# Parts of queries and keys stored once in memory, and picked for the stacks by the loads

## The reference

```python
q, k, v = (heads(w, b) for w, b in ((wq, bq), (wk, bk), (wv, bv)))   # 16 heads of D = 16
q, k = _apply_rope(q, cos, sin), _apply_rope(k, cos, sin)            # turns the two halves of D
att = softmax(causal(einsum('bhtd,bhsd->bhts', q, k) / sqrt(D)))
y = einsum('bhts,bhsd->bhtd', att, v)
x = layernorm(x + y @ wp.T + bp)
x = layernorm(x + experts(x))      # 32 experts, 8 of them per token, weighted
```

## Time and profile before

| | |
|---|---|
| median of 3 runs | 2250.6 us (2250.48 to 2256.99) |
| the profiled execution | span 2243.6 us; no other time of it is given |
| TensorE matmuls busy | 1846.1 us (82%) |
| VectorE busy | 1604.2 us (71%) |
| ScalarE busy | 1324.9 us (59%) |
| GpSimd busy | 1247.5 us (56%) |
| DMA, all queues | 520.20 MB in 290572 packets, mean 232 GB/s |
| granted TensorE clock, mean | 0.918 |

### The profile page before, as it was taken

The page is one execution under the profiler, slowest core; times in us unless marked ns, Lnnn a source line. Parts: engine busy times, 40 slices in busy tenths (PEclk is TensorE's granted clock), DMA queues, the critical chain, the costliest instruction groups (busy, mean ns, idle before and its releaser), DMA issues.

```text
span 2243.6 us, 54153 instructions
## 1 busy us (share of the span) xinstructions
PE 1846.1 (82%) x17104; PEld 1323.3 (59%) x17104; DVE 1604.2 (71%) x3572; ACT 1324.9 (59%) x2865; POOL 1247.5 (56%) x1206
## 2 busy tenths in 40 slices
PE   4898888998889888988878989899878889887740
PEld 2555554555545454555446878787767777776630
DVE  4888877887788777877854545575467778776688
ACT  1566565655554554655446767777766667775630
POOL 1004446444644465444644777777777777775660
PEclk7999999999999999999989999999989999998865
DMA  5466577667766876556676766656789988887887
GB/s 164 149 181 222 191 232 248 222 192 227 256 217 200 264 246 226 190 189 222 216 237 219 229 178 214 209 187 199 213 299 307 302 289 299 262 289 266 283 283 256
DMA packets 290572, 520.20 MB, mean 232 GB/s; under 512 B 46329, under 2 KB 192192, under 8 KB 280529
## 3 DMA queue, kind: packets, MB, share of 16 engines
q1 hardware_dynamic: 206400, 324.46, 47.5%
q0 software_dynamic: 58368, 163.70, 19.7%
q10 hardware_dynamic: 25536, 28.58, 3.8%
HBM read 284.54 MB, written 259.20 MB: 242 GB/s over the span
## 4 chain that ended last, share of the span: by engine, by line
PE 39%; DVE 20%; DMA 20%; issue 9%; ACT 5%; SPq 4%; POOL 2%; ACTq 1%; DVEq 1%; POOLq 0%
DMA xTden<-reciprocals 7%; DVE mn L1649 5%; PE ps L1016 4%; PE ps L1094 4%; PE ps L1041 3%; PE ps L1135 3%; PE ps L1067 3%; PE ps L1154 3%; PE ps L1081 3%; PE ps L1137 3%; PE ps L1136 3%; PE ps L1200 2%; PE ps L965 2%; DMA out<-x1T 1%; POOL y_tokens L898 1%
## 5 line engine op out<-in xcount | busy, mean ns | idle before, releaser
L1292 ACT ACTIVATE pT<-ps 128x512 f32<-128x512 f32 (+2 forms) x1008 | 679.5, 703 | 438.3 <-PE ps L1069 315.9
L880 POOL DMA_INDIRECT x_sorted<-xhl,idx x512 | 529.6, 1034 | 508.4 <-DVE xhl L1724 229.3
L1649 DVE TENSOR_REDUCE mn<-ps 128x1 f32<-128x512 f32 (+3 forms) x704 | 412.5, 631 | 55.5 <-PE ps L1043 53.0
L1135 PE MATMUL ps<-pT,gu_hi 128*128 128x256 f16 (+1 forms) x1600 | 383.1, 255 | 23.7 <-ACT pT L1292 12.3
L1136 PE MATMUL ps<-pT,gu_hi 128*128 128x256 f16 (+1 forms) x1600 | 381.9, 254 | 0.0
L1137 PE MATMUL ps<-pT,gu_lo 128*128 128x256 f16 (+1 forms) x1600 | 381.8, 254 | 0.0
L898 POOL DMA_INDIRECT y_tokens<-work,yidx x264 | 283.3, 1073 | 94.8 <-issue 59.1
L1041 PE MATMUL ps<-stacks 96*128 96x512 bf16 (+3 forms) x1024 | 275.4, 312 | 46.6 <-DVE mn L1649 25.4
L1067 PE MATMUL ps<-stacks 99*128 99x512 bf16 (+3 forms) x1024 | 286.5, 311 | 15.1 <-ACT pT L1292 10.1
L1069 PE MATMUL ps<-maskk,identb 128*128 128x128 bf16 x1024 | 223.0, 224 | 0.0
L1200 PE MATMUL ps<-dn,vx 128*128 x608 | 172.0, 283 | 53.0 <-DVE cosT L1857 13.4
(11 more groups left out here) (299 smaller groups left out, 3780.9 us busy)
## 6 DMA issues: line engine op xcount, KB each, us to landing
stacks<-y_tokens SPq DMA_DIRECT2D x64, 1024.0 KB
stacks<-qk_parts SPq DMA_DIRECT2D x128, 384.0 KB
qk_parts<-pbuf SPq DMA_DIRECT2D x62, 384.0 KB
attention<-yev ACTq DMA_DIRECT2D x64, 256.0 KB
qk_parts<-pbuf SPq DMA_DIRECT2D x62, 256.0 KB
stacks<-x_sorted SPq DMA_DIRECT2D x52, 304.0 KB, 4.0
x_sorted<-pads_h SPq DMA_DIRECT2D x99, 152.0 KB
pbuf<-x_sorted SPq DMA_DIRECT2D x40, 304.0 KB
```

The costliest lines, as they stand in the source:

```text
L880: pool.indirect_dma_start(xsort[g][:, :], bass.IndirectOffsetOnAxis(ap=at, axis=0), xhl_rows[:, t, :], None).then_inc(s_scat, 16)
L1135: mmul(o, w_hi[k], x_hi[k], start=k == 0, stop=False)
L1292: return nc.scalar.activation(o, i, f, **k)
L1649: V.tensor_reduce(mn[:, tt, h0:h0 + nh], ps[:, odd_bank("max", at, m), 0:nh * n].rearrange("p (a n) -> p a n", a=nh), axis=AX.X, op=ALU.ma ...
```

## The change

The memory tensor holds the three parts of D = 16 dimensions once, as rows ordered by part, half and j, and in each row the 16 heads side by side. A partition of the tiles is now (j, head) instead of (head, j): weights, biases and the tables of cosines and sines are loaded or built in that order. The parts tile has the part outside and the halves inside; keys have their parts in the reverse order (part_column). One DMA writes the parts of a batch's queries or keys. The stack is loaded by three DMAs of three, two and one part (48, 32 and 16 partitions); for queries they begin at part 0, for keys they end at the last column. A partition's four heads of 512 tokens lie together in memory and in the tile. Counts of s_qkw and s_stk follow.

```diff
-    parts_dram = nc.dram_tensor("qk_parts", [B, 2, H * KS, T], BF16, kind="Internal").ap()
+    parts_dram = nc.dram_tensor("qk_parts", [B, 2, 3 * D, H, T], BF16, kind="Internal").ap()
...
-        pbuf = sb("pbuf", [P, 2, 3, T], BF16)
+        pbuf = sb("pbuf", [P, 3, 2, T], BF16)
...
+        def part_column(n, part):
+
+            return (part, 2 - part)[n]
...
-                        sp.dma_start(dst[:, r:r + 1], src.rearrange("(h r j o) -> r h j o", h=H, r=2, o=1)[r]).then_inc(s_cst, 16)
+                        sp.dma_start(dst[:, r:r + 1], src.rearrange("(h r j o) -> r j h o", h=H, r=2, o=1)[r],
+                                     allow_slow_non_contiguous=True).then_inc(s_cst, 16)
...
-                                 src.rearrange("(h r j) c -> r h j c", h=H, r=2)[r]).then_inc(s_wnat, 16)
+                                 src.rearrange("(h r j) c -> r j h c", h=H, r=2)[r]).then_inc(s_wnat, 16)
...
                 if g == 0:
-                    wait(sp, s_qkw, 192 * (b + 1))
+                    wait(sp, s_qkw, 32 * (b + 1))
                 wait(sp, s_st, NU * (m - 2))
                 for n, dst in enumerate((qs, ks)):
-                    sp.dma_start(dst[0:KS, r, :, :],
-                                 parts_dram[b, n, 4 * KS * g:4 * KS * (g + 1), :].rearrange("(h k) t -> k h t", h=4)).then_inc(s_stk[r], 16)
+                    at = 0
+                    for count in (3, 2, 1):
+                        first = (0, 3 - count)[n]
+                        sp.dma_start(dst[at * D:(at + count) * D, r, :, :],
+                                     parts_dram[b, n, first * D:(first + count) * D, 4 * g:4 * g + 4, :]).then_inc(s_stk[r], 16)
+                        at += count
...
-                runs = (((0, 3, 0), (3, 2, 0), (5, 1, 0)), ((0, 3, 0), (3, 2, 1), (5, 1, 2)))[n]
                 wait(sp, s_pp, 2 * b + n + 1)
-                dst = parts_dram[b, n].rearrange("(p r a) t -> r p a t", r=2, a=6)
-                for half in range(2):
-                    for at, count, part in runs:
-                        src = parts(b, n)[:, half, part:part + count, :] if n == 0 else \
-                            parts(b, n)[:, half, part:part + 1, :].to_broadcast([P, count, T])
-                        sp.dma_start(dst[half][:, at:at + count, :], src).then_inc(s_qkw, 16)
+                sp.dma_start(parts_dram[b, n].rearrange("(q j) h t -> (j h) q t", q=6),
+                             parts(b, n).rearrange("p a r t -> p (a r) t")).then_inc(s_qkw, 16)
...
-                actv(parts(b, n)[:, :, part, :], rotated(b, n)[:, :, :], ACT.Copy).then_inc(s_part, 1)
+                actv(parts(b, n)[:, part_column(n, part), :, :], rotated(b, n)[:, :, :], ACT.Copy).then_inc(s_part, 1)
...
-    rows = np.tile(ang.T, (H, 1))
+    rows = np.repeat(ang.T, H, axis=0)
```

More of the change, by code:

```diff
@@ L452, in build @@
         rcp = prep[:, 3 * C + 3 * E + 4:3 * C + 3 * E + 8].rearrange("p (r m) -> p r m", r=2)
-        first_parts = pT[1][:, :, :].rearrange("p h t -> p (h t)").bitcast(BF16).rearrange("p (r a t) -> p r a t", r=2, a=3)
+        first_parts = pT[1][:, :, :].rearrange("p h t -> p (h t)").bitcast(BF16).rearrange("p (a r t) -> p a r t", r=2, a=3)
         wv_nat, wp_nat = (pT[0][:, k, :].rearrange("p (m c) -> p m c", m=2) for k in range(2))
@@ L461, in build @@
         row_homes = [(qs.rearrange("p r h t -> p (r h t)"), 5), (ks.rearrange("p r h t -> p (r h t)"), 5),
-                     (flat(pT[1][:, :, :]), 2), (pbuf[:, :, :, :].rearrange("p r a t -> p (r a t)"), 2),
+                     (flat(pT[1][:, :, :]), 2), (pbuf[:, :, :, :].rearrange("p a r t -> p (a r t)"), 2),
                      (flat(xTden[:, :, :]), 1), (flat(ynum[:, :, :]), 1), (flat(qf[:, :, :]), 1), (flat(x1[:, :, :]), 1),
@@ L1036, in max_unit @@
                 if m == 0:
-                    wait(pe, s_stk[r], 32 * (at // 3 + 1))
+                    wait(pe, s_stk[r], 96 * (at // 3 + 1))
                 k = odd.take(s_red, NM * at + m + 1, "max", at, m)
@@ L1362, in part_copy @@
                     if b > 0:
-                        wait(act, s_qkw, 96 * at)
+                        wait(act, s_qkw, 16 * at)
                 else:
                     wait(act, s_rest, at + 1)
-                actv(parts(b, n)[:, :, part, :], rotated(b, n)[:, :, :], ACT.Copy).then_inc(s_part, 1)
+                actv(parts(b, n)[:, part_column(n, part), :, :], rotated(b, n)[:, :, :], ACT.Copy).then_inc(s_part, 1)
             def values(b, v):
@@ L1634, in rest @@
                 q = rotated(b, n)[:, :, :]
-                V.tensor_tensor(q, q, parts(b, n)[:, :, 0, :], ALU.subtract).then_inc(s_rest, 1)
+                V.tensor_tensor(q, q, parts(b, n)[:, part_column(n, 0), :, :], ALU.subtract).then_inc(s_rest, 1)
             def last_part(b, n):
@@ L1641, in last_part @@
                 wait(dve, s_part, part_count(b, n, 1))
-                V.tensor_tensor(parts(b, n)[:, :, 2, :], rotated(b, n)[:, :, :], parts(b, n)[:, :, 1, :],
+                V.tensor_tensor(parts(b, n)[:, part_column(n, 2), :, :], rotated(b, n)[:, :, :], parts(b, n)[:, part_column(n, 1), :, :],
                                 ALU.subtract).then_inc(s_pp, 1)
```

## The result

The changed kernel takes 2230.1 us (median of 6 runs) against 2250.7 for the one before (6 runs): ratio 0.9919, 95% interval 0.9894 to 0.9945. In a second comparison, with 10 and 13 runs, it was 2236.2 against 2245.3: 0.9952, interval 0.9921 to 0.9982. Both say faster, by 0.8 and 0.5%; the forecast was 2228 and 2206 to 2247. The forecast gain was 22.7 us. The first comparison shows 20.6 and the second 9.1, less than half of it; over all runs on record, 32 of the kernel before and 16 of the changed one, the means differ by 14 us, give or take 4.

The account below looks back on a forecast made before the run. No engine fills the kernel; late reciprocals, the chain's largest item, hold VectorE's division. Gains of 17.9 + 3.8 - 1 + 2 = 22.7 us off 2250.6 give 2228 us, range 2206 to 2247.

Parts of the forecast that it names:

- Backlog ahead of the numerators: Attention batches: queued writes and loads delay the numerators by 2.2 us; clearing them gives 1.9 a batch, 17.9 us in all.
- the keys' side: Next batch's stack loads go out about 3 us sooner after the keys' halved write; 2 us gained.
- 0.85 and 0.6: Batch time saved per us of less waiting at VectorE's division: 0.85 in the first nine batches, 0.6 in five later.
- rival C: TensorE's clock: moved idle stretches bring slow ones, 2268 us; against it, fewer or shorter slow stretches, 2218; chance 0.07.
- The start: Before the first stack matmul: halved writes land 3.8 us sooner, weights loaded in the new order cost 1 us.
- the weights' order: Queries' and keys' weights read with j ahead of h at the start: 0 to 1.7 us slower, 1 taken.
- The loads: Stack loads by pieces ahead of the numerators: 3.3 us a pair, as before; bounds 2.0 and 6.6 us.
- A: Loads by pieces take 6 us or more a pair and eat the gain, 2249 us; A or nothing: 0.13.
- B: Scatters and weights fill the DMA engines instead; a third of the 17.9 us remains, 2240 us; chance 0.17.
- D: The transfer of 10 us shrinks too and the 14 waits at the division vanish whole, 2210 us; chance 0.08.
- the signs I named: New profile: 241 thousand packets, 495 MB, seven issues before rotation's end, division waits about 30 us, first stacks' wait about 14.
- one sign of being wrong: At the numerators' issue in each batch: the forecast is wrong if 4 KB packets still run then.

Follow-up runs that it names:

- swap2: Changed kernel with the reciprocals' loads issued ahead of the numerators': 2206.3 us, attention phase 1104.1 us.
- rows_1k: Changed kernel with 128 bytes of padding behind each head's row, so loads have 1 KB packets again while writes stay halved: attention phase 1133.6 us.

## Why the prediction was right

The mechanism, a backlog ahead of the numerators, was right and is shown. That the sum came so near is in part luck: sizes inside it were off in opposite directions, and the second comparison gives only 9.1 us. The profiles, from their start to the first expert load, give 20.2 us (1201.2 against 1181.0, means of two).

*Backlog ahead of the numerators, 17.9 us.* The place and the mechanism held. The attention phase is 1154.8 before and 1136.4 after (means of two), 18.4 us less, this term and the keys' side together, of which I had forecast 19.9. But two sizes inside were off, in opposite directions. I took 0.7 us as the shortest time from issue to first packet, from the empty window behind a write's issue (that write's first packet came at 0.87); for these loads it is 1.4, in both kernels' first batch and in twelve of the next thirteen of the changed one. So the shift was not 1.9 us a batch but 1.3, the mean over the 13 batches behind the first (2.75 to 1.45 us), and the waits fell by 13.2 us (means of two), where I had 24 before the factors. Against that, I multiplied by 0.85 and 0.6, each read from one pair of batches, and the phase fell by more than the waits, not less. What the waits don't explain is of the size of a fall in TensorE's busy time. The attention phase in one window, before and after (us, busy and count of PE, PEld, DVE, ACT, POOL, then granted clock, DMA share, GB/s):

```profile
44.50:1200.00 1155.50, 1001.15 (x7935) 591.84 (x7935) 905.75 (x2192) 641.31 (x1248) 509.03 (x507) 0.94 0.66 213
```
```profile
42.90:1178.70 1135.80, 995.36 (x7935) 587.84 (x7935) 905.68 (x2192) 640.76 (x1249) 511.11 (x507) 0.95 0.61 196
```

The same 7,935 matmuls are busy 5.8 us less, at a mean granted clock of 0.95 for 0.94. In swap2 they take 976.4 us at 0.96. The traces' records of the granted clock show as many stretches at 1.2 GHz in the phase as before, 27 and 26 for 26 and 26, but shorter ones: 125 and 117 us in all, for 150 and 141 (swap2: 17 stretches, 81 us). It went the way I had named as the case against rival C, with about half the size. That the clock is the cause of the whole remainder is argued from these rows, not tested by itself.

*The start, 3.8 - 1.* Queries' parts were ready 1.5 us later (issue at 30.92 for 29.39); most of it is the price of the weights' order, for which I had 1 and the wait shows 1.7 in this pair. The two writes landed 5.6 us behind it instead of 9.4: 3.8 us, as forecast. The loads then took 6.4 us to the first stack matmul instead of 5.7, where I had put no change. The sum is 1.6 us sooner in the first pair of profiles, 2.1 in the second, for 2.8. By itself that would prove little, since the same kernel's first stack matmul moves by 3.4 to 3.9 us from one profile to the other; but the 5.6 and 9.4 us repeat in both pairs.

*The loads, 3.3 us a pair.* At 219 GB/s it is 3.6. The Trainium skill's rule of ports (SBUF — State Buffer, Door 1: The DMA port swizzle) would have made it 4.8, an estimate, with the pieces one after another. The rows agree with it in that 96 partitions are filled well below the writes' 384 GB/s, whatever the packet (though these are also loads against writes), and not with most of the further loss: the three pieces seem to overlap for the greater part. Which ports were used isn't shown.

*The keys' side, 2.* The waits for stacks behind the first are 2.2 us for 3.3, so 1.1, and 1.4 for 2.6 in the second pair, 1.2.

*The rivals.* A is out by the issue times and rows_1k. B, that other queues would fill the engines, doesn't show: the first packet comes 1.4 us behind the issue, as into the queue of the first batch, and the transfers did not get longer. They did not get shorter either (9.3 us from the first to the last packet before, 9.5 after, means over 13 batches), so D didn't come. C is out for this change. Of the signs I named, traffic, issues and TensorE's first wait came out. The waits at the division are 42 us where I had said about 30, and the numerators' packets start 1.4 us behind their issue, not 0.7. And one sign of being wrong is there: 4 KB packets still run when the numerators are issued, 34 of them in the batch above and 4 to 97 in each of the first 15. It was too strict a sign. Where fewer than 35 of them are left, the first packet comes at 1.42 to 1.46 us all the same; with 56 and 97 left it comes at 1.52 and 2.66.

## What to carry to other kernels

Find the transfer that stands on the chain and add up the bytes that are queued ahead of it, between what frees its issue and its first packet: these count, and the same bytes 16 us later in the batch cost a tenth. When the queue is nearly empty there, look again at the order of the issues: an edit that gave 5 us in front of a full queue gave 32 after it. And read the attention phase or its like from two fixed instructions when executions scatter by more than the change is worth.

## What the runs showed of the hardware that I had not expected

The numerators' load had its first packet 1.4 us behind its issue, in nearly every batch, where the writes from tiles to memory at the start showed theirs at 0.9. The direction is not the reason: the stack loads at the start, from memory too and into an empty queue, showed theirs at 0.94 to 1.00 us. The issues differ in length, 0.66 us for a load of numerators, 0.36 for the write and 0.33 for the stack load, which is more than half of the difference; what makes the rest stays open. Stack loads took as long in 4 KB packets as in 1 KB packets, and a little longer in three pieces than in one. And the same instructions, with the same inputs, took 1043.5 and 1057.2 us in the expert phase of two executions of one kernel; what decides that stays open.
